# A two-direction Mamba layer and its FFN on one core: the order of convolution, projections and turned steps

## The chip, the cores and the metric

The kernel runs on one core of a Trainium2 chip. TensorE (PE in the profile, PEld its weight loads), VectorE (DVE), ScalarE (ACT), GpSimd (POOL) and SyncE (SP, here the DMA queue) each work off their own instruction stream and wait for each other with semaphores. The metric is the device time of one execution in microseconds (us), the median of several.

## What is computed

The input x has 4 sequences of 512 tokens with 128 features. It is normalised, a Mamba block runs over it forwards and over its reverse, both results are added, normalised again and added to x; then an FFN with int weights (hidden size 384) follows in the same sandwich of layer norms. One Mamba pass, with inner size 256 and 16 states:

```python
xz = einsum('bld,ed->ble', x, in_w); u, z = split(xz, 2)
u = silu(causal depthwise conv of u with 4 taps + conv_b)
x_dbl = einsum('bld,ed->ble', u, xproj_w)      # 8 columns for dt, 16 for B, 16 for C
dt = softplus(x_dbl[..., :8] @ dt_w.T + dt_b)
dA = exp(dt[..., None] * A); dBu = dt[..., None] * B[:, :, None, :] * u[..., None]
h_t = dA_t * h_(t-1) + dBu_t;  y_t = sum over the 16 states of h_t * C_t
y = (y + u * D) * silu(z);  out = y @ out_w.T
```

## The kernel before, in words

**Units and steps.** A unit k is one sequence q = k // 2 in one direction d = k % 2: eight units (UNITS). Each has 16 steps, one for each state (NS); step i of the 128 belongs to unit i // 16 and has position i % 16. A step works on tiles of 128 partitions by 1024: the two halves of the inner size side by side, 512 tokens each. For a step, ScalarE makes the decay `da` with two exponentials (stage "exp"), VectorE runs one scan instruction over decay and input `bb` (stage "scan"), GpSimd multiplies the result `hq` by the row of C (stage "mul_c"), and TensorE sums the state over all 16 steps into the PSUM tile `ysum` by eight transposing matmuls (stage "fold", three slots later, FOLD_LAG).

**Three kinds of step.** They differ in how the input dt * B * u comes about. In a plain step TensorE broadcasts the row of B into PSUM with one matmul ("bcast") and VectorE multiplies it by `dtu` ("mul_b"). In a turned step (table TURNED) ScalarE scales the transposed `dtu_t` by B's columns with four activations ("g") and TensorE turns it back with eight transposes ("g_turn"), so that VectorE has only the scan. In a pooled step (table POOLED) GpSimd does the product from a row of B that a DMA spread over the partitions ("mul_b_pooled"), and ScalarE writes the decay into the PSUM tile ("exp_psum", line 909 on). There are two such PSUM tiles (BB_RING), so the feed of step i + 1 waits for scan i - 1. `da` has six buffers and `hq` five. Scan i also waits for fold i - 5.

**The order.** `plan()` writes one list, ORDER, by hand. Slot i holds scan i, mul_c i, the feed of step i + 1, the exponentials of step i + 5, the stages in `sooner[i]`, fold i - 3, and then those that `put(slot, ...)` appended to `woven[i]`. Slots in the table `late` have their exponentials after the woven stages of the slot named there. Every engine walks through the same list and executes its own stages, so the place in the list is the place in each engine's stream. Between the steps of a unit are woven:

- four taps for each of two halves of the next unit's convolution ("tap", TensorE, line 781), which is done with in-projection weights multiplied by the taps, then "conv_out" (ScalarE, Silu, line 963), which leaves `u` in one of three buffers (U_RING);
- "z" (two matmuls, Silu, line 970); "xproj" (two matmuls, copied to `xdbl`), whose B and C rows SyncE stores to DRAM and loads again, spread, as `c_tiles` and `b_tiles`; "bc", "split" (GpSimd, four small operations) and "b_rows", which prepare B; "dt" (two matmuls, Softplus, line 993) and "dtu" (GpSimd), "dtu_turn" (transposes);
- for the unit that has just ended, "y_out" (ScalarE, slot 2, copies `ysum`), "back" (TensorE adds the skip term and turns y into token order, lines 743 and 748) and "gate" (VectorE multiplies it by `zs`, line 1381);
- in even units from 2 on, out-projection and layer norm 2 of the sequence before; in odd ones from 3 on layer norm 3 and the FFN of it ("ln_square", "ln_var", "ln_pow", "ln_shift", "ln_act", "turn_x1", "ffn_gate", "ffn_up", "ffn_down"). I call these FFN units.

Exp, Silu and Softplus need different activation tables of ScalarE; a table load appears in the profile at the line of the activation behind it.

**Scratch.** All woven matmuls write to two PSUM banks (`scr`). `plan_banks` walks the list and gives each result the bank whose last use ends first, from its first matmul to the stage that reads it; `may_write` makes TensorE wait until the previous holder of the bank has been read.

The stages of unit k before, as offsets to its first slot: taps of unit k + 1 in 0 to 3 with both conv_outs in 3; z in 4; back in 5 and 6, gates in 6 and 7; xproj in 7, bc in 8, dt, split and dtu in 9; b_rows in 10 or 11; FFN gates in 10 and 11. Unit 0 has its convolution three slots later.

Of the kernel before, what the change touches and what calls it, by code (L numbers as in the profile page):

```python
# [27 lines left out]
UNITS = 2 * SEQS  # L28
# [26 lines left out]
TURNED = ((4, 6, 10, 13), (2, 4, 6, 10, 13)) + 3 * ((3, 6, 10, 12, 15), (0, 5, 10, 13))  # L55
POOLED = ((15,), (15,), (8, 14), (15,)) + 2 * ((8, 14), (8, 15))
# [60 lines left out]
def plan():  # L117
# [26 lines left out]
    late = {}  # L144
    for k in range(UNITS):
        q, d, n, at = k // 2, k % 2, k + 1, NS * k
        more, ffn = n < UNITS, d == 1 and q >= 1
        lag = 3 if k == 0 else 0
        g_slot = {2: 0, 3: 0, 4: 1, 5: 1, 6: 2, 10: 6, 12: 9, 13: 8 if ffn else 10, 15: 11}
# [3 lines left out]
        for p in POOLED[k]:  # L153
            put(at + {8: 4, 14: 10, 15: 11}[p], ("mul_b_pooled", at + p))
# [9 lines left out]
        if more:  # L164
            put(at + lag, *taps(n, 0)[:2])
            put(at + lag + 1, *taps(n, 0)[2:])
            put(at + lag + 2, *taps(n, 1)[:2])
            put(at + lag + 3, *taps(n, 1)[2:], ("conv_out", n, 0), ("conv_out", n, 1))
        put(at + lag + 4, ("z", k, 0), ("z", k, 1))
        late[at + lag + 4] = at + lag + 4  # L170

        if k >= 1:
            put(at + 5, ("back", k - 1, 0))
            put(at + 6, ("gate", k - 1, 0), ("back", k - 1, 1))
            put(at + 7, ("gate", k - 1, 1))

        if more:
            then = 1 if k == 0 else 0
            put(at + then + 7, ("xproj_mm", n, 0), ("xproj_mm", n, 1), ("xproj", n))
            put(at + then + 8, ("bc", n))  # L180
            put(at + then + 9, ("dt_mm", n, 0), ("dt_mm", n, 1), ("dt", n, 0), ("dt", n, 1), ("split", n), ("dtu", n))

        if d == 0 and q >= 1:
            for b in range(BLK):
                put(at + 10 + b, ("oproj_mm", q - 1, 0, b))
            put(at + 13, ("oproj", q - 1, 0))
            put(at + 14, ("ln_square", 2, q - 1))
            put(at + 15, ("ln_var", 2, q - 1, 0), ("ln_pow", 2, q - 1, 0))
            put(at + 16, ("ln_act", 2, q - 1, 0), ("add_attn", q - 1, 0))
            put(at + 18, ("ln_square", 3, q - 1))  # L190
            put(at + 19, ("ln_var", 3, q - 1, 0), ("ln_pow", 3, q - 1, 0), ("ln_shift", 3, q - 1, 0))
            put(at + 21, ("ln_act", 3, q - 1, 0))
        if ffn:
            soon = 0 if more else -2
            put(at + soon + 7 + 2 * (not more), ("turn_x1", q - 1, 0))
            put(at + soon + 10, ("ffn_gate", q - 1, 0, 0), ("ffn_gate", q - 1, 0, 1))
            put(at + soon + 11, ("ffn_gate", q - 1, 0, 2))
            late[at + soon + 10] = late[at + soon + 11] = at + soon + 11
# [10 lines left out]
        if more:  # L209
            put(at + (11 if ffn or k == 0 else 10), ("b_rows", n))  # L210
            soon = 1 if d == 0 and k >= 1 else 0
            put(at + 12 - soon, ("dtu_turn", n, 0))
            put(at + 13 - soon, ("dtu_turn", n, 1))
            if q < LAST:
                put(at + 14, ("turn", q + 1, d))
            if 0 in TURNED[n]:
                put(at + 14 - soon, ("g", at + NS))
# [8 lines left out]
    for i in range(STEPS + FOLD_LAG):  # L226
        if i < STEPS:
# [5 lines left out]
            if i + 1 < STEPS and not is_turned(i + 1) and not is_pooled(i + 1):  # L233
                order.append(("mul_b", i + 1))
            if i not in late:
                order += exps(i)
            order += sooner[i]
# [79 lines left out]
def mamba_sandwich(nc, x, packed, conv_taps, w_u, w_ffn, bc_rows, out):  # L317
# [3 lines left out]
    with ExitStack() as ctx:  # L321
# [252 lines left out]
        def _(sp):  # L574
# [13 lines left out]
            for k in range(UNITS):  # L588
# [4 lines left out]
                for m in range(NS // 2):  # L593
# [8 lines left out]
                    for p in POOLED[k]:  # L602
                        if m == {8: 0, 14: 3, 15: 3}[p]:
# [896 lines left out]
```

## Time and profile before

| | |
|---|---|
| time, median of 3 | 470.99 us (468.65 to 473.14) |
| profiled execution | 472.82 us, its span 471.0 us |
| mean granted clock of TensorE | 0.921 of full |
| PE busy | 405.1 us (86%) |
| DVE busy | 422.3 us (90%) |
| ACT busy | 374.3 us (79%) |
| POOL busy | 398.9 us (85%) |
| DMA | 42.6 MB on one hardware queue, 26.4% of 16 engines |

The first scan starts at 23.1 us and the last ends at 439.7; the scans of the units begin at 23.1, 77.1, 126.8, 175.8, 231.0, 278.8, 335.0 and 382.8. What follows the last scan is the last sequence's projection, norms and FFN. In the rows below a stretch A:B is given in us from the span's start, then its length, then for each engine busy us and in brackets the instructions, then TensorE's granted clock as a share of full speed, the DMA engines' share and GB/s. In the time order a line has start, duration, engine, source line, operation and tiles, number of instructions merged, and in square brackets the idle time ahead with what ended it.

### The profile page before, as it was taken

How to read it: one execution, taken by the hardware profiler on the slowest of the kernel's cores; microseconds unless marked ns; L12 is line 12 of the kernel's file. 1: busy time of each engine (PE TensorE's matmuls, PEld its weight loads, DVE VectorE, ACT ScalarE, POOL GpSimd, SP SyncE). 2: the span in 40 equal slices, each digit the busy share in tenths (PEclk: the TensorE clock that was granted, in tenths of full speed). 3: DMA queues.
4: the chain of work that ended last, by engine and by line, in shares of the span. 5: the costliest groups of instructions: out<-in, count | busy, mean ns of one | idle time of the engine just before them, and what ended most of it. 6: DMA issues, size and time to landing. Idle time of an engine off the chain costs nothing. (4 is left out here: it accounts for less than half of the span.)

```text
span 471.0 us, 6668 instructions
## 1 busy us (share of the span) xinstructions
PE 405.1 (86%) x2250; PEld 277.5 (59%) x2250; DVE 422.3 (90%) x338; ACT 374.3 (79%) x732; POOL 398.9 (85%) x239
## 2 busy tenths in 40 slices
PE   7759898997699799789998899889998965879973
PEld 3346476555456684555656775455766854548853
DVE  3998989999999999899999999988999999889744
ACT  4798799798858997998889997997889887863330
POOL 1678999978999799979989999979789999968421
PEclk9958958998899999999999999979998995979978
DMA  8531112322232213231233323122322223210001
GB/s 244 205 147 61 75 66 102 131 82 81 82 118 90 96 46 113 89 97 67 94 110 110 118 89 114 61 100 94 112 87 93 96 89 113 90 45 1 2 0 45
DMA packets 17777, 43.02 MB, mean 91 GB/s; under 512 B 1616, under 2 KB 7120, under 8 KB 17744
## 3 DMA queue, kind: packets, MB, share of 16 engines
q1 hardware_dynamic: 17744, 42.61, 26.4%
q8 instruction: 18, 0.29, 0.3%
q14 instruction: 15, 0.12, 0.1%
HBM read 41.03 MB, written 1.57 MB: 90 GB/s over the span
## 5 line engine op out<-in xcount | busy, mean ns | idle before, releaser
L1123 POOL TENSOR_TENSOR hq<-hq,c_tiles 128x1024 f32<-128x1024 f32 x127 | 298.0, 2366 | 30.6 <-DVE hq L1276 30.3
L1276 DVE TENSOR_TENSOR_SCAN hq<-da,bb 128x1024 f32<-128x1024 f32 x115 | 260.4, 2280 | 9.4 <-PE bb L679 2.9
L909 ACT ACTIVATE da<-dt,neg_a 128x511 f32<-128x511 f32 x230 | 149.8, 711 | 7.4 <-DVE hq L1276 7.2
L707 PE MATMUL ysum<-wts,hq 128*128 128x128 f32 x1024 | 145.9, 290 | 7.7 <-ACT y_t L949 4.9
L707 PEld LDWEIGHTS ysum<-wts,hq 128*128 128x128 f32 x1024 | 121.6, 148 | 32.6 <-issue 19.7
L1257 DVE TENSOR_TENSOR bb<-bb,dtu 128x1024 f32<-128x1024 f32 x79 | 95.8, 1213 | 8.3 <-PE bb L652 7.5
L1020 ACT ACTIVATE g<-dtu_t,bc_t 128x256 f32<-128x256 f32 x144 | 61.0, 498 | 0.0
L679 PE MATMUL bb<-wts,g 128*128 128x128 f32 x288 | 43.2, 300 | 8.0 <-ACT g L1020 5.7
L679 PEld LDWEIGHTS bb<-wts,g 128*128 128x128 f32 x288 | 36.4, 154 | 17.6 <-issue 10.2
L652 PE MATMUL bb<-b_rows,pick 48*128 48x512 bf16 x75 | 29.9, 398 | 10.2 <-DVE hq L1276 10.2
L1276 DVE TENSOR_TENSOR_SCAN hq<-bb,dbu 128x1024 f32<-128x1024 f32 x13 | 29.7, 2281 | 6.7 <-issue 4.3
L652 PEld LDWEIGHTS bb<-b_rows,pick 48*128 48x128 bf16 x75 | 7.0, 93 | 45.1 <-issue 22.5
L781 PE MATMUL scr<-xn_rev,wconv 128*128 128x512 f32 x64 | 32.3, 628 | 0.0
L1135 POOL TENSOR_TENSOR dbu<-dtu,b_tiles 128x1024 f32<-128x1024 f32 x13 | 30.8, 2367 | 0.0
L873 PE MATMUL scr<-x_t,wffn 128*128 128x512 f32 (+1 forms) x46 | 24.5, 639 | 5.3 <-issue 2.7
L781 PE MATMUL scr<-xn_fwd,wconv 128*128 128x512 f32 x56 | 27.1, 609 | 0.0
L1225 POOL TENSOR_TENSOR rstd<-rstd,minus_half 128x4 f32<-128x4 f32 (+1 forms) x15 | 13.8, 922 | 15.0 <-DVE rstd L1397 14.3
L909 ACT ACT_TABLE_LOAD x17 | 21.8, 1283 | 0.4
L970 ACT ACTIVATE zs<-scr 128x512 f32<-128x512 f32 x16 | 9.6, 598 | 12.0 <-PE scr L791 12.0
L791 PE MATMUL scr<-xn_fwd,wts 128*128 128x512 f32 x32 | 15.2, 597 | 2.7 <-ACT u L963 2.7
L781 PEld LDWEIGHTS scr<-xn_rev,wconv 128*128 128x128 f32 x64 | 11.8, 206 | 9.4 <-issue 9.4
L1212 POOL TENSOR_TENSOR dtu<-dt,u 128x1024 f32<-128x1024 f32 x7 | 16.5, 2362 | 0.6 <-ACT dt L993 0.5
(150 smaller groups left out, 489.8 us busy)
## 6 DMA issues: line engine op xcount, KB each, us to landing
c_tiles<-bc_rows_dram SPq DMA_DIRECT2D x64, 512.0 KB, 3.6
b_tiles<-bc_rows_dram SPq DMA_DIRECT2D x13, 256.0 KB, 4.4
x_res<-x_dram SPq DMA_DIRECT2D x1, 768.0 KB, 8.1
out_dram<-o SPq DMA_DIRECT2D x3, 256.0 KB, 2.3
wts<-packed_dram SPq DMA_DIRECT2D x1, 584.0 KB, 9.1
hid<-w_ffn_dram SPq DMA_DIRECT2D x1, 576.0 KB, 7.8
wconv<-conv_taps_dram SPq DMA_DIRECT2D x2, 256.0 KB, 4.4
wconv<-conv_taps_dram SPq DMA_DIRECT2D x1, 512.0 KB, 7.6
```

The lines of the kernel that those rows point to most:

```text
L652: mm = nc.tensor.matmul(bb[:, i % BB_RING, 1, :], pick[0:PARTS * NS, n:n + 1].broadcast_to([PARTS * NS, P]), b_rows[:, k % 2, :], start=Tr ...
L679: mm = nc.tensor.matmul(bb[:, i % BB_RING, h, block(b)], g[:, n % G_RING, b, h, :], ident, start=True, stop=True, is_transpose=True)
L707: mm = nc.tensor.matmul(ysum[:, bank, at], hq[:, i % H_RING, h, block(b)], ident, start=opens, stop=(i % NS == NS - 1), is_transpose=True, ...
L781: mm = nc.tensor.matmul(scratch(use), wconv[:, d, t, h * P:(h + 1) * P], src, start=(t == 0), stop=(t == TAPS - 1))
L873: signal_full(nc.tensor.matmul(scratch(use)[:, 0:at.stop - at.start], w[:, block(c)], x1_t[:, at], start=True, stop=True), use)
L909: ins = nc.scalar.activation(da[:, i % DA_RING, h, 1:SEQ], dt[:, k % 2, h, 1:SEQ], ACT.Exp, scale=neg_a[:, c:c + 1])
L1020: ins = nc.scalar.activation(g[:, m % G_RING, b], dtu_t[:, k % 2, b], ACT.Copy, scale=bc_t[:, k % 2, b, ROW_B + n:ROW_B + n + 1])
L1123: nc.gpsimd.tensor_tensor(hq[:, i % H_RING], hq[:, i % H_RING], c_tiles[:, n % C_RING, i % 2, :].unsqueeze(1).broadcast_to([P, 2, SEQ]), A ...
L1135: nc.gpsimd.tensor_tensor(dbu[:], dtu[:, k % 2], b_tiles[:, n % POOLED_RING].unsqueeze(1).broadcast_to([P, 2, SEQ]), ALU.mult).then_inc(s_ ...
L1212: nc.gpsimd.tensor_tensor(dtu[:, k % 2], dt[:, k % 2], u[:, k % U_RING], ALU.mult).then_inc(s_dtu, 1)
L1257: nc.vector.tensor_tensor(bb[:, i % BB_RING], bb[:, i % BB_RING, 1, :].unsqueeze(1).broadcast_to([P, 2, SEQ]), dtu[:, k % 2], ALU.mult).th ...
L1276: nc.vector.tensor_tensor_scan(out=hq[:, i % H_RING].rearrange("p h t -> p (h t)"), data0=decay.rearrange("p h t -> p (h t)"), data1=dbu_t ...
```

## The change

The tables have six turned steps a unit from unit 2 on (3, 5, 7, 10, 12, 15 in even units, 0, 3, 5, 7, 10, 13 in odd ones) and one pooled step (14 or 15). The convolution of unit k + 2 is put into slots 3 to 6 of unit k, for k from 2 to 5; unit 0 makes that of unit 1, unit 1 those of units 2 and 3. From unit 2 on xproj is in slot 0, bc and split in slot 1, b_rows in slot 2, back in slots 3 and 4, gates in 4 and 5, z in slot 7, and dt in slot 8, or 9 in FFN units. There the exponentials of slots 7 to dt's come behind dt. The FFN gates stand in slots 8 and 9, the turn of x1 in `sooner` of slot 7, which now comes ahead of the slot's exponentials, and LN 3's stages in slots 3, 4 and 6. The transposes of x and their evaluation ("turn") move to an earlier unit accordingly. SyncE loads the row of the pooled step behind the fourth pair of C rows in all units.

```diff
--- before.py
+++ after.py
@@ -52,8 +52,8 @@
 PARTS = 3
-TURNED = ((4, 6, 10, 13), (2, 4, 6, 10, 13)) + 3 * ((3, 6, 10, 12, 15), (0, 5, 10, 13))
-POOLED = ((15,), (15,), (8, 14), (15,)) + 2 * ((8, 14), (8, 15))
+TURNED = ((4, 6, 10, 13), (2, 4, 6, 10, 13)) + 3 * ((3, 5, 7, 10, 12, 15), (0, 3, 5, 7, 10, 13))
+POOLED = ((15,), (15,)) + 3 * ((14,), (15,))
 POOLED_RING = 2
@@ -142,16 +142,23 @@
                           (3 * NS + 9, "attn_in", 3)):
         put(slot, (name, q))
     late = {}
+
+    def conv_ahead(slot, n):
+
+        put(slot, *taps(n, 0)[:2])
+        put(slot + 1, *taps(n, 0)[2:])
+        put(slot + 2, *taps(n, 1)[:2])
+        put(slot + 3, *taps(n, 1)[2:], ("conv_out", n, 0), ("conv_out", n, 1))
+
     for k in range(UNITS):
         q, d, n, at = k // 2, k % 2, k + 1, NS * k
         more, ffn = n < UNITS, d == 1 and q >= 1
-        lag = 3 if k == 0 else 0
-        g_slot = {2: 0, 3: 0, 4: 1, 5: 1, 6: 2, 10: 6, 12: 9, 13: 8 if ffn else 10, 15: 11}
+        g_slot = {2: 0, 3: 0, 4: 1, 5: 2, 6: 2, 7: 4, 10: 6 if k < 2 else 5, 12: 9, 13: 10, 15: 11}
         for p in TURNED[k]:
             if p:
                 put(at + g_slot[p], ("g", at + p))
         for p in POOLED[k]:
-            put(at + {8: 4, 14: 10, 15: 11}[p], ("mul_b_pooled", at + p))
+            put(at + {14: 10, 15: 11}[p], ("mul_b_pooled", at + p))
         if k == 0:
             put(at, ("dtu_turn", 0, 0), ("dtu_turn", 0, 1), ("pick",), ("split", 0), ("turn", 0, 1))
             put(at + 1, ("b_rows", 0))
@@ -161,41 +168,46 @@
             put(at + 8, ("down_sum",))
             put(at + 11, ("down_centre",))
+        if k <= 1:
+            conv, z_slot, back, xproj, bc = (at + 2 - 2 * k, at + 6 - 2 * k, at + 5, at + 7 - 2 * k, at + 8 - k)
+            conv_ahead(conv, n)
+        else:
+            z_slot, back, xproj, bc = at + 7, at + 3, at, at + 1
+        dt_slot = at + (9 if k == 0 else 10 if k == 1 else 9 if ffn else 8)
+        put(z_slot, ("z", k, 0), ("z", k, 1))
+        if k <= 1:
+            late[z_slot] = z_slot
+            if k == 1:
+                late[dt_slot] = dt_slot
+        else:
+            for s in range(at + 7, dt_slot + 1):
+                late[s] = dt_slot
+
+        if k >= 1:
+            put(back, ("back", k - 1, 0))
+            put(back + 1, ("gate", k - 1, 0), ("back", k - 1, 1))
+            put(back + 2, ("gate", k - 1, 1))
+        if k >= 1 and k + 2 < UNITS:
+            conv_ahead(at + (6 if k == 1 else 3), k + 2)
+
         if more:
-            put(at + lag, *taps(n, 0)[:2])
-            put(at + lag + 1, *taps(n, 0)[2:])
-            put(at + lag + 2, *taps(n, 1)[:2])
-            put(at + lag + 3, *taps(n, 1)[2:], ("conv_out", n, 0), ("conv_out", n, 1))
-        put(at + lag + 4, ("z", k, 0), ("z", k, 1))
-        late[at + lag + 4] = at + lag + 4
-
-        if k >= 1:
-            put(at + 5, ("back", k - 1, 0))
-            put(at + 6, ("gate", k - 1, 0), ("back", k - 1, 1))
-            put(at + 7, ("gate", k - 1, 1))
-
-        if more:
-            then = 1 if k == 0 else 0
-            put(at + then + 7, ("xproj_mm", n, 0), ("xproj_mm", n, 1), ("xproj", n))
-            put(at + then + 8, ("bc", n))
-            put(at + then + 9, ("dt_mm", n, 0), ("dt_mm", n, 1), ("dt", n, 0), ("dt", n, 1), ("split", n), ("dtu", n))
-
+            put(xproj, ("xproj_mm", n, 0), ("xproj_mm", n, 1), ("xproj", n))
+            put(bc, ("bc", n), ("split", n))
         if d == 0 and q >= 1:
             for b in range(BLK):
                 put(at + 10 + b, ("oproj_mm", q - 1, 0, b))
             put(at + 13, ("oproj", q - 1, 0))
             put(at + 14, ("ln_square", 2, q - 1))
             put(at + 15, ("ln_var", 2, q - 1, 0), ("ln_pow", 2, q - 1, 0))
-            put(at + 16, ("ln_act", 2, q - 1, 0), ("add_attn", q - 1, 0))
-            put(at + 18, ("ln_square", 3, q - 1))
-            put(at + 19, ("ln_var", 3, q - 1, 0), ("ln_pow", 3, q - 1, 0), ("ln_shift", 3, q - 1, 0))
-            put(at + 21, ("ln_act", 3, q - 1, 0))
+            put(at + 17, ("ln_act", 2, q - 1, 0), ("add_attn", q - 1, 0))
         if ffn:
+            put(at + 3, ("ln_square", 3, q - 1))
+            put(at + 4, ("ln_var", 3, q - 1, 0), ("ln_pow", 3, q - 1, 0), ("ln_shift", 3, q - 1, 0))
+            put(at + 6, ("ln_act", 3, q - 1, 0))
             soon = 0 if more else -2
-            put(at + soon + 7 + 2 * (not more), ("turn_x1", q - 1, 0))
-            put(at + soon + 10, ("ffn_gate", q - 1, 0, 0), ("ffn_gate", q - 1, 0, 1))
-            put(at + soon + 11, ("ffn_gate", q - 1, 0, 2))
-            late[at + soon + 10] = late[at + soon + 11] = at + soon + 11
+            sooner[at + 7].append(("turn_x1", q - 1, 0))
+            put(at + 8, ("ffn_gate", q - 1, 0, 0), ("ffn_gate", q - 1, 0, 1))
+            put(at + 9, ("ffn_gate", q - 1, 0, 2))
             for c in range(3):
                 sooner[at + soon + 12 + c].append(("ffn_up_mm", q - 1, 0, c))
                 put(at + soon + 12 + c, ("ffn_up", q - 1, 0, c))
@@ -207,12 +219,16 @@
             put(at + soon + 20, ("ln_act", 4, q - 1, 0), ("add_ffn", q - 1, 0))
         if more:
-            put(at + (11 if ffn or k == 0 else 10), ("b_rows", n))
+            put(dt_slot, ("dt_mm", n, 0), ("dt_mm", n, 1), ("dt", n, 0), ("dt", n, 1), ("dtu", n))
+            put(at + (2 if k >= 2 else 11), ("b_rows", n))
             soon = 1 if d == 0 and k >= 1 else 0
             put(at + 12 - soon, ("dtu_turn", n, 0))
-            put(at + 13 - soon, ("dtu_turn", n, 1))
-            if q < LAST:
-                put(at + 14, ("turn", q + 1, d))
+            put(at + 13, ("dtu_turn", n, 1))
+            if k == 0:
+                put(at + 13, ("turn", 1, 0))
+                put(at + 14, ("turn", 1, 1))
+            elif k + 3 < UNITS:
+                put(at + 14, ("turn", (k + 3) // 2, (k + 3) % 2))
             if 0 in TURNED[n]:
                 put(at + 14 - soon, ("g", at + NS))
     put(STEPS - 5, ("oproj_part_mm",), ("oproj_part",))
@@ -232,9 +248,9 @@
                 order.append(("g_turn" if is_turned(i + 1) else "exp_psum" if is_pooled(i + 1) else "bcast", i + 1))
             if i + 1 < STEPS and not is_turned(i + 1) and not is_pooled(i + 1):
                 order.append(("mul_b", i + 1))
+            order += sooner[i]
             if i not in late:
                 order += exps(i)
-            order += sooner[i]
         f = i - FOLD_LAG
         last_in_slot = f >= NS and f % NS == 0
@@ -600,7 +616,7 @@
                                                                                       ).partition_broadcast(P)
                                  ).then_inc(s_cl[n % C_RING], 16)
                     for p in POOLED[k]:
-                        if m == {8: 0, 14: 3, 15: 3}[p]:
+                        if m == 3:
                             n = pooled_steps(NS * k + p)
                             if n >= POOLED_RING:
```

## Rows read from the trace of the kernel before

**Rows 1.** Stretches (units 4, 5): us; PE, PEld, DVE, ACT, POOL busy; clock; DMA.

```profile
231.00:279.00 48.00, 44.08 (x287) 32.10 (x286) 46.33 (x27) 43.16 (x89) 46.03 (x26) 1.00 0.31 105
...
279.00:335.00 56.00, 51.33 (x265) 31.95 (x263) 51.53 (x33) 49.20 (x97) 53.01 (x32) 0.94 0.29 96
```

**Rows 2.** Groups by line on the page: busy us, mean ns, idle before.

```profile
L1020 ACT ACTIVATE g<-dtu_t,bc_t 128x256 f32<-128x256 f32 x144 | 61.0, 498 | 0.0
...
L1135 POOL TENSOR_TENSOR dbu<-dtu,b_tiles 128x1024 f32<-128x1024 f32 x13 | 30.8, 2367 | 0.0
...
L909 ACT ACT_TABLE_LOAD x17 | 21.8, 1283 | 0.4
```

**Rows 3.** Waits of VectorE: engine, line, releaser; us, times, longest.

```profile
DVE bb L1257 <- PE bb L652: 7.5, 9, 1.9
...
DVE hq L1276 <- issue: 4.3, 3, 1.8
...
DVE hq L1276 <- ACT bb L920: 2.4, 3, 0.9
```

**Rows 4.** VectorE in order of time: start us, us, what, idle before.

```profile
138.56 1.23 DVE L1257 TENSOR_TENSOR bb<-bb,dtu 128x1024 f32<-128x1024 f32 x1 [0.29 <-PE bb L652]
...
196.20 1.23 DVE L1257 TENSOR_TENSOR bb<-bb,dtu 128x1024 f32<-128x1024 f32 x1 [1.90 <-PE bb L652]
...
297.79 1.23 DVE L1257 TENSOR_TENSOR bb<-bb,dtu 128x1024 f32<-128x1024 f32 x1 [0.54 <-PE bb L652]
...
299.12 2.29 DVE L1276 TENSOR_TENSOR_SCAN hq<-da,bb 128x1024 f32<-128x1024 f32 x1
...
301.32 1.21 DVE L1257 TENSOR_TENSOR bb<-bb,dtu 128x1024 f32<-128x1024 f32 x1
...
302.43 0.68 DVE L1381 TENSOR_TENSOR gated<-scr,zs 128x512 f32<-128x512 f32 x1
...
307.67 2.29 DVE L1276 TENSOR_TENSOR_SCAN hq<-bb,dbu 128x1024 f32<-128x1024 f32 x1 [1.78 <-issue]
...
320.02 1.23 DVE L1257 TENSOR_TENSOR bb<-bb,dtu 128x1024 f32<-128x1024 f32 x1 [0.77 <-PE bb L652]
...
324.19 0.69 DVE L1432 TENSOR_TENSOR hid<-scr,hid 128x512 f32<-128x512 f32 x1 [0.56 <-PE scr L873]
```

**Rows 5.** TensorE in order of time, unit 5.

```profile
285.81 0.39 PE L652 MATMUL bb<-b_rows,pick 48*128 48x512 bf16 x1
...
286.13 1.09 PE L707 MATMUL ysum<-wts,hq 128*128 128x128 f32 x8
...
287.06 1.88 PE L781 MATMUL scr<-xn_fwd,wconv 128*128 128x512 f32 x4
...
288.87 0.39 PE L652 MATMUL bb<-b_rows,pick 48*128 48x512 bf16 x1
...
292.84 1.04 PE L679 MATMUL bb<-wts,g 128*128 128x128 f32 x8
...
293.71 1.04 PE L707 MATMUL ysum<-wts,hq 128*128 128x128 f32 x8
...
298.61 1.02 PE L743 MATMUL scr<-u,skip_diag 128*128 128x512 f32 x2
...
300.01 0.39 PE L652 MATMUL bb<-b_rows,pick 48*128 48x512 bf16 x1
```

**Rows 6.** ScalarE in order of time, unit 5.

```profile
294.65 1.26 ACT L963 ACTIVATE u<-scr,wts 128x512 f32<-128x512 f32 x2
...
298.08 1.28 ACT L909 ACT_TABLE_LOAD   x1
...
299.38 2.56 ACT L909 ACTIVATE da<-dt,neg_a 128x511 f32<-128x511 f32 x4
...
301.84 1.64 ACT L1055 ACTIVATE ln_tile<-x_res,shift,rstd 128x128 f32<-128x128 f32 x4
```

**Rows 7.** The emptiest stretch of TensorE in unit 7, same columns as rows 1.

```profile
389.00:395.00 6.00, 1.65 (x10) 0.90 (x9) 5.82 (x4) 5.50 (x13) 6.00 (x4) 0.58 0.47 131
```

## The prediction

> **What bounds the kernel now.** I read the stretches by unit first, because the program is eight units of sixteen steps and an average over the span hides which unit has slack. In the stretch of unit 4 VectorE is busy 46.3 of 48 us, in unit 5 51.5 of 56 [rows 1]. GpSimd follows at 46.0 and 53.0. So the even units already run at VectorE's pace; what is left is idle time of VectorE in the odd ones. A step costs VectorE one scan, 2.20 us from its start to the next instruction's, and a plain step a product more, 1.3 us (297.79 to the scan at 299.12); a gate adds 0.6, its 0.68 less the overlap [rows 4].
>
> The groups by line give the prices [rows 2], the list of waits says what VectorE waits for [rows 3]: broadcasts of B by TensorE (7.5 us in nine waits), decays that ScalarE writes into PSUM for a pooled step (2.4 in three), and 4.3 us in three waits without a releaser. The time order places them [rows 4]: 1.90 us in unit 3 and 0.54 in unit 5, both at step 6, right behind the slots that hold convolution and z; 0.29 at the same step of unit 2; 0.77 in unit 5 behind the first FFN matmuls and 0.56 at the first up product; 1.78 ahead of the pooled step 8 of unit 5, one of the three without releaser.
>
> **Work removed from VectorE.** Counting the tables, turned steps go from 36 to 45, pooled from 13 to 8, plain from 79 to 75. Four products fewer on the engine that sets the pace, at 1.3 us: **-5.2 us** (two in unit 3, one each in 5 and 7).
>
> **Pooled step 8 goes.** All three waits without releaser stand ahead of step 8 (units 2, 5, 7). The product by GpSimd had long been ready, so I read them as ScalarE being late with a decay that cannot be made ahead, since it needs one of the two PSUM tiles. **-4.3 us.** Step 14 stays pooled in even units, and so do its waits (2.4); I leave them, and put them at nought only in the low case. GpSimd loses five products of 2.367 us, 11.8 in all; it sets no VectorE wait in rows 3, so I count nothing, but it is what gives GpSimd room for the shorter odd units: 53.0 busy of 56 in unit 5 would otherwise stand above VectorE's.
>
> **ScalarE.** A turned step needs four scalings: 144 took 61.0 us, so 1.69 us a step, and nine more are +15.2. A pooled step's two exponentials cost what a plain one's do. Table loads take 1.283 us each [rows 2]; the 17 into Exp stand there. By the order, before, a unit with a successor has Silu, Exp, Softplus, Exp (4), an FFN unit one more Silu, unit 7 four; that is 34. After, units 0 and 1 have 4 and 5, units 2 to 6 three each (Silu, Softplus, Exp), unit 7 two: 26. Eight fewer are -10.3. Net +4.9 us on an engine busy 43.2 of 48 and 49.2 of 56 [rows 1]. Hidden by VectorE's 48 us; nothing. If that cover were gone, 0.7 us a unit.
> The row shows a load starting at 298.08 and the next exponential at 299.38, 1.30 us later [rows 6]. The Trainium skill (ScalarE: Activation LUTs, What ACT_TABLE_LOAD costs) adds a drain of about 1.38 us to each switch. By it eight loads would be worth 21 us and ScalarE would end with less work than before. Here the row decides: no such drain is seen.
>
> **TensorE, where the change costs.** Nine more turns back at 0.87 us (292.84 to 293.71) against four broadcasts of 0.32: about +6.6 us of work, but its place matters more. Pitches from start to start [rows 5]: broadcast 0.32 (285.81), fold 0.93 (286.13), two taps 1.81 (287.06), back 1.40 (298.61 to 300.01), turn 0.87. Today taps lie in slots 0 to 3 and back in 5 to 7. From unit 2 on, slots 3 to 6 hold both, and two of the steps fed there, 5 and 7, become turned, so that the slots before them are short. Slot 3: 0.32+0.93+1.40+1.81 = 4.5. Slot 4: 0.87+0.87+1.40+1.81 = 5.0. Slot 5: 0.32+0.93+1.81 = 3.1. Slot 6: 0.87+0.87+1.81 = 3.6. Sum 16.1. VectorE's time in the same slots, scans of 2.2, two products (1.3), two gates (0.6): 3.5+2.8+4.1+2.2 = 12.6. TensorE can run behind by one scan (2.2 us) before VectorE waits, because two PSUM tiles alternate. From the start of scan 3 to the product of step 8 VectorE has 14.8 us of work; TensorE's broadcast for it is done at 16.1+0.4. So at least **1.7 us** of waiting in each of units 2 to 5.
> There are also waits inside. Scratch has two banks. With the taps of half 0 holding one from slot 3 to 6, back of half 1 must wait until VectorE's gate of half 0 has read the other (slot 4), and the taps of half 1 until the gate of half 1 has (slot 5). Followed from scan 3 at 0: turn for step 5 done at 5.2, back 1 from 6.3, broadcast 6 at 9.8, so the product of step 6 starts 1.4 late; its gate ends at 11.8, taps until 13.6, turn 7 at 14.5 (0.6 late); broadcast 8 at 17.4 (0.7 late). **2.7 us** a unit, four units: **+10.8**. I take this one, since the gates' waits follow from the order. It replaces 1.90, 0.54 and 0.29 [rows 4]: **-2.7**. Behind the waiting matmul on TensorE stand the next feed and fold, so VectorE is the one who waits.
>
> **FFN units.** x1 is now turned early in slot 7, and its input, LN 3's scaling, stands on ScalarE behind the second conv_out. A Silu half is 0.6 us, the scaling 1.64 [rows 6]: TensorE sits some 2.1 us, then x1's turn (0.6), fold, z (1.81) and the broadcast follow: step 9's product starts 2.2 us late. Dt behind three gate matmuls in slot 9 may add 1.1. Units 3 and 5: **+4.4** (between 0 and +6.6). It replaces waits behind the FFN matmuls in unit 5, 0.77 and 0.56: **-1.3**. Unit 7 has no convolution; its waits I leave.
>
> **Smaller moves.** xproj in slot 0, bc and split in slot 1, b_rows in slot 2 lie where no taps are now: 0.32+0.93+1.81 is under a plain slot's 3.5. SyncE's store of the rows stands behind the unit's C loads in its queue as before, so it moves at most a few us earlier; split moves past GpSimd's products of slots 2 to 9 and adds none. Nothing for either. Postponed exponentials of slots 7 to 9 are those of steps 12 to 14, needed three slots later: nothing. Units 0 and 1 get other slots at the same work: nothing, +-1.
>
> **Sum.** -5.2 -4.3 -2.7 -1.3 +10.8 +4.4 = +1.7 us. The profiled execution took 472.8 us for its span of 471.0; the median of the runs is 471.0. 471.0+1.7: **472.7, called 472.5**.
>
> **Rivals.**
> *TensorE keeps up* (faster). If only the unavoidable 1.7 a unit shows (+6.8) and the x1 turn is on time (0): -13.5+6.8 = -6.7, 464; with step 14's waits gone as well, -9.1, 462. For it: ScalarE loses loads and GpSimd a product a unit, and folds could then fall in earlier. Against it: both stalls come from the written order, not from a loaded engine. Chance 0.31.
> *The dense stretch costs its full price* (slower). One mechanism: TensorE in slots 3 to 9 of units 2 to 5. With dt's 1.1 also paid (+2.2) and slots 3 and 4 partly run at half rate, 1.7 us a unit (+6.8), +10.7: 481. It decides from about 1.5 us more a unit than my 2.7. The clock side is seen in the trace: in 389 to 395 TensorE is busy 1.65 of 6 us and the granted clock is 0.58 of full, that is part of it at 1.2 in place of 2.4 GHz [rows 7]; the taps that fill slots 0 to 2 today leave them, and slot 1 will hold 1.7 us of 3.5. Against it: xproj and b_rows fill some, and the drop at 389 came after emptier slots. Chance 0.27.
> The Trainium skill (TensorE: Matmul & The Clock Gate, HAM oscillation) says that an array left idle for a while between bursts goes back to half rate and starts each burst cold. The stretch of [rows 7] agrees for unit 7; for units 2 to 5 it would give the 481, and I put 0.10 of the 0.27 on it.
> *The change does not do what it says* (a bank or a semaphore serialises TensorE so that the visits of ScalarE are split again): then loads stay near 34 and the time lies within the slower case.
>
> **Numbers.** Forecast (within 1%, about what a measurement of this kernel can tell from no change) 0.42, its own range 467 to 475.5; faster 0.31; slower 0.27, the third rival inside it. Range 461 to 480: the low end is the first rival's full case, the high end cuts the last of the second's.
>
> **What would show it.** Right: VectorE waits for TensorE's broadcast at steps 6 and 8 and its turn at 7 in units 2 to 5, some 2.7 us together, and at step 9 in units 3 and 5; TensorE's weight loads waiting for `gated`; 45 turned groups, 8 fewer table loads; no wait ahead of step 8. Wrong: units 2 to 5 shorter than before with no waits in slots 5 to 9 (TensorE had more room than the pitches say), or a clock below 1.0 in slots 3 to 6, or waits for GpSimd's C products, which would make it the bound of units 3 and 5.

## The result and the profile after

The changed kernel takes **499.3 us** (median; 498.9 to 500.1) against 471.0; the ratio is 1.060 (95% interval 1.055 to 1.066). The forecast was 472.5, its range 461 to 480, with 0.27 on slower. The profiled execution has a span of 497.2 us, 26.2 more than before.

Busy time by engine, part 1 of the page of the kernel after (us, share of the span, instructions):

```profile
PE 418.4 (84%) x2318; PEld 288.9 (58%) x2318; DVE 418.9 (84%) x334; ACT 378.1 (76%) x755; POOL 388.0 (78%) x234
```

No engine has much more work: VectorE 3.4 us less, GpSimd 10.9 less, ScalarE 3.8 more, TensorE 13.3 more. So the 26 us are idle time of the engine that sets the pace. Groups by line on the same page, which answer to [rows 2]; the number behind the bar's second place is the idle time ahead:

```profile
L1139 POOL TENSOR_TENSOR hq<-hq,c_tiles 128x1024 f32<-128x1024 f32 x127 | 298.4, 2367 | 62.2 <-DVE hq L1292 62.1
...
L925 ACT ACTIVATE da<-dt,neg_a 128x511 f32<-128x511 f32 x240 | 156.2, 715 | 2.7 <-DVE hq L1292 2.5
...
L1273 DVE TENSOR_TENSOR bb<-bb,dtu 128x1024 f32<-128x1024 f32 x75 | 91.1, 1215 | 29.3 <-PE bb L668 29.2
L1036 ACT ACTIVATE g<-dtu_t,bc_t 128x256 f32<-128x256 f32 x180 | 76.6, 503 | 1.6 <-PE bb L695 1.1
...
L1151 POOL TENSOR_TENSOR dbu<-dtu,b_tiles 128x1024 f32<-128x1024 f32 x8 | 19.0, 2372 | 0.0
```

The counts are those forecast: 75 products, 180 scalings (45 steps), 8 pooled products. Table loads fell from 39 to 31, into Exp from 17 to this:

```profile
L925 ACT ACT_TABLE_LOAD x11 | 14.1, 1283 | 0.3
```

GpSimd waits twice as long for VectorE (62.1 us) as before, so it is further from setting the time. The list of waits of VectorE and of TensorE in the kernel after (us in total, times, longest), to be held against [rows 3]:

```profile
DVE bb L1273 <- PE bb L668: 29.2, 24, 3.2
DVE hid L1448 <- PE scr L889: 8.4, 2, 4.2
DVE hq L1292 <- PE bb L695: 6.5, 6, 2.3
```

```profile
PE bb L695 <- ACT g L1036: 17.5, 9, 5.2
PE scr L682 <- POOL b_parts L1216: 10.4, 6, 2.7
PE scr L797 <- DVE gated L1397: 3.9, 4, 1.0
```

I then went along VectorE's time order and added its idle times of 0.2 us and more between the first and the last scan, by unit and by step:

| waits of VectorE, us | before | after |
|---|---|---|
| unit 0; unit 1 | 3.6; 0.3 | 0.3; 4.5 |
| steps 4 to 8 of units 2 to 5, but for pooled steps | 2.7 | 21.3 |
| step 9 of units 3 and 5 | 0 | 5.2 |
| step 11 of units 3 and 5 | 0 | 3.2 |
| steps 12 and 13 of units 2 to 6 | 1.8 | 15.5 |
| pooled steps 8; 14 | 4.3; 2.4 | 0; 0 |
| unit 7 without its pooled step | 3.8 | 0.4 |
| step 0 of unit 5 | 0 | 0.4 |
| sum | 18.9 | 50.7 |

31.8 more waits less 5.2 of products are 26.6; from the first to the last scan it took 27.7 us more, and the tail 1.3 less. The units took, before, 54.0, 49.7, 49.0, 55.2, 47.8, 56.2, 47.8 and (to the last scan's start) 54.7 us; after, 49.9, 54.5, 56.0, 64.4, 54.5, 66.1, 49.4 and 47.3. So units 1 to 6 lose 39.1 us and the two ends give back 11.5.

Unit 4 after, VectorE in order of time (start us, us, what, idle before), where [rows 4] has such rows of before:

```profile
260.36 2.29 DVE L1292 TENSOR_TENSOR_SCAN hq<-da,bb 128x1024 f32<-128x1024 f32 x1
262.56 0.67 DVE L1397 TENSOR_TENSOR gated<-scr,zs 128x512 f32<-128x512 f32 x1
264.69 2.29 DVE L1292 TENSOR_TENSOR_SCAN hq<-da,bb 128x1024 f32<-128x1024 f32 x1 [1.46 <-PE bb L695]
268.85 1.23 DVE L1273 TENSOR_TENSOR bb<-bb,dtu 128x1024 f32<-128x1024 f32 x1 [1.87 <-PE bb L668]
...
273.74 2.29 DVE L1292 TENSOR_TENSOR_SCAN hq<-da,bb 128x1024 f32<-128x1024 f32 x1 [0.87 <-issue]
276.59 1.23 DVE L1273 TENSOR_TENSOR bb<-bb,dtu 128x1024 f32<-128x1024 f32 x1 [0.57 <-PE bb L668]
```

These are scan 5, the product of step 6, scan 7 and the product of step 8: the places forecast, at 1.87, 0.87 and 0.57 for 1.4, 0.6 and 0.7, and 1.46 at step 5 that was not. TensorE shows where that one begins, in slot 2:

```profile
257.23 0.40 PE L682 MATMUL scr<-ident,b_parts 128*48 128x128 bf16 x4 [1.68 <-POOL b_parts L1216]
...
257.88 1.73 PE L759 MATMUL scr<-u,skip_diag 128*128 128x512 f32 x2
259.41 1.06 PE L764 MATMUL scr<-wts,y_t 128*128 128x128 f32 x4
```

It stands at b_rows until GpSimd has split B, the broadcast for step 4 queued behind it, and the back that follows takes 2.4 us in place of 1.4. The clock was granted at half (1.2 of 2.4 GHz) for a part of this stretch:

```profile
256.00:262.00 6.00, 4.77 (x14) 2.55 (x15) 5.91 (x4) 6.00 (x14) 5.69 (x8) 0.72 0.23 87
```

Unit 5 after, ScalarE, TensorE and VectorE around steps 11 to 13:

```profile
345.87 1.09 ACT L1009 ACTIVATE dt<-scr 128x512 f32<-128x512 f32 x2
...
346.98 1.28 ACT L925 ACT_TABLE_LOAD   x1
...
348.27 3.78 ACT L925 ACTIVATE da<-dt,neg_a 128x511 f32<-128x511 f32 x6
...
351.96 1.69 ACT L1036 ACTIVATE g<-dtu_t,bc_t 128x256 f32<-128x256 f32 x4
...
353.70 1.97 PE L695 MATMUL bb<-wts,g 128*128 128x128 f32 x8 [4.12 <-ACT g L1036]
...
357.48 0.69 DVE L1448 TENSOR_TENSOR hid<-scr,hid 128x512 f32<-128x512 f32 x1 [4.22 <-PE scr L889]
```

Dt is late, the table load follows, then the three postponed pairs of exponentials, and only then the scaling for step 13. (Slot 10 has no pair of its own, since step 15 is pooled here.) TensorE waits 4.1 us for the scaling, with the FFN's up matmul behind the turn in its queue, and VectorE 4.2 us for that matmul. The granted clock is 0.67 of full from 345 to 351 us and 0.50 from 351 to 357, and the turn behind the wait takes 1.97 us where one at full clock took 1.04 [rows 5]. The profile names the FFN at the end of this chain; its cause is ScalarE's order.

### The profile page after: what moved, and what is told of

It reads as the page before. It is cut to its first block and busy times, and to the rows that moved or that the text cites. A ratio compares the mean times of both kernels' runs of the same rounds, so it can differ in the third digit from the quotient of the medians.

```text
span 497.2 us, 6835 instructions
## 1 busy us (share of the span) xinstructions
PE 418.4 (84%) x2318; PEld 288.9 (58%) x2318; DVE 418.9 (84%) x334; ACT 378.1 (76%) x755; POOL 388.0 (78%) x234
## 5 line engine op out<-in xcount | busy, mean ns | idle before, releaser
L1139 POOL TENSOR_TENSOR hq<-hq,c_tiles 128x1024 f32<-128x1024 f32 x127 | 298.4, 2367 | 62.2 <-DVE hq L1292 62.1
L1292 DVE TENSOR_TENSOR_SCAN hq<-da,bb 128x1024 f32<-128x1024 f32 x120 | 272.2, 2281 | 18.4 <-PE bb L695 6.5
L925 ACT ACTIVATE da<-dt,neg_a 128x511 f32<-128x511 f32 x240 | 156.2, 715 | 2.7 <-DVE hq L1292 2.5
L1273 DVE TENSOR_TENSOR bb<-bb,dtu 128x1024 f32<-128x1024 f32 x75 | 91.1, 1215 | 29.3 <-PE bb L668 29.2
L1036 ACT ACTIVATE g<-dtu_t,bc_t 128x256 f32<-128x256 f32 x180 | 76.6, 503 | 1.6 <-PE bb L695 1.1
L695 PE MATMUL bb<-wts,g 128*128 128x128 f32 x360 | 52.9, 295 | 25.5 <-ACT g L1036 17.5
L695 PEld LDWEIGHTS bb<-wts,g 128*128 128x128 f32 x360 | 44.0, 151 | 38.4 <-ACT g L1036 26.1
L979 ACT ACTIVATE u<-scr,wts 128x512 f32<-128x512 f32 x16 | 10.8, 687 | 23.4 <-PE scr L797 21.5
L1151 POOL TENSOR_TENSOR dbu<-dtu,b_tiles 128x1024 f32<-128x1024 f32 x8 | 19.0, 2372 | 0.0
L1292 DVE TENSOR_TENSOR_SCAN hq<-bb,dbu 128x1024 f32<-128x1024 f32 x8 | 18.2, 2271 | 0.4 <-ACT bb L936 0.4
L1024 ACT ACTIVATE dtu_t<-scr 128x512 f32<-128x512 f32 x16 | 9.4, 591 | 11.2 <-PE scr L703 11.2
```

The costliest lines, as they stand in the source:

```text
L695: mm = nc.tensor.matmul(bb[:, i % BB_RING, h, block(b)], g[:, n % G_RING, b, h, :], ident, start=True, stop=True, is_transpose=True)
L925: ins = nc.scalar.activation(da[:, i % DA_RING, h, 1:SEQ], dt[:, k % 2, h, 1:SEQ], ACT.Exp, scale=neg_a[:, c:c + 1])
L1036: ins = nc.scalar.activation(g[:, m % G_RING, b], dtu_t[:, k % 2, b], ACT.Copy, scale=bc_t[:, k % 2, b, ROW_B + n:ROW_B + n + 1])
L1139: nc.gpsimd.tensor_tensor(hq[:, i % H_RING], hq[:, i % H_RING], c_tiles[:, n % C_RING, i % 2, :].unsqueeze(1).broadcast_to([P, 2, SEQ]), A ...
L1151: nc.gpsimd.tensor_tensor(dbu[:], dtu[:, k % 2], b_tiles[:, n % POOLED_RING].unsqueeze(1).broadcast_to([P, 2, SEQ]), ALU.mult).then_inc(s_ ...
L1273: nc.vector.tensor_tensor(bb[:, i % BB_RING], bb[:, i % BB_RING, 1, :].unsqueeze(1).broadcast_to([P, 2, SEQ]), dtu[:, k % 2], ALU.mult).th ...
```

## Experiments

Each run names a theory that the trace after had not settled. The two main ones: **order** (where the stages stand) and **tables** (nine more turned steps load TensorE and ScalarE).

**Order alone.** The order after, the tables before; the product of the pooled step 8 is then in slot 4 and its row of B is loaded first, as before:

```diff
-TURNED = ... + 3 * ((3, 5, 7, 10, 12, 15), (0, 3, 5, 7, 10, 13))
+TURNED = ... + 3 * ((3, 6, 10, 12, 15), (0, 5, 10, 13))
-POOLED = ((15,), (15,)) + 3 * ((14,), (15,))
+POOLED = ((15,), (15,), (8, 14), (15,)) + 2 * ((8, 14), (8, 15))
```

Expected: 

> The order of the changed kernel with the step tables of the kernel before (36 turned, 13 pooled, 79 plain). Theory 'order': the loss comes from where convolution, back, gates, dt and the postponed exponentials stand, so the kernel stays slow, 488 to 502 us; it has 5.2 us more products on VectorE but longer slots. Theory 'tables': the nine extra turned steps load TensorE and ScalarE; without them it is near the kernel before, 468 to 476 us.

Measured: 507.0 us, ratio to before 1.080 (1.072 to 1.089). Worse than the whole change, and above the range given for either theory; so in the new order the new tables are worth 7.7 us. The waits at steps 4 to 7 are there, and the pooled steps 8 wait far longer than in [rows 4], since ScalarE's exponentials for them now follow conv_out and, in unit 5, LN 3's scaling (unit 5, VectorE; in units 2 and 4 it is 2.58 us each):

```profile
343.65 2.29 DVE L1292 TENSOR_TENSOR_SCAN hq<-bb,dbu 128x1024 f32<-128x1024 f32 x1 [4.10 <-ACT bb L936]
```

**Tables alone.** The order before, the tables after (in the kernel before); the scaling for step 7 is put into slot 4:

```diff
-TURNED = ... + 3 * ((3, 6, 10, 12, 15), (0, 5, 10, 13))
+TURNED = ... + 3 * ((3, 5, 7, 10, 12, 15), (0, 3, 5, 7, 10, 13))
-POOLED = ((15,), (15,), (8, 14), (15,)) + 2 * ((8, 14), (8, 15))
+POOLED = ((15,), (15,)) + 3 * ((14,), (15,))
```

Expected: 

> The order of the kernel before with the new step tables (45 turned, 8 pooled, 75 plain). Theory 'order': near the kernel before, 463 to 474 us (5.2 us of products and 4.3 us of waits at step 8 gone, some waits for TensorE added). Theory 'tables': most of the 28 us loss is here, 488 us or more.

Measured: 471.7 us, ratio 1.003 (0.999 to 1.006). So the loss is the order's. But in the old order the tables bring nothing either: what they take from VectorE comes back largely where ScalarE's scaling for step 3 is late in odd units, with TensorE behind it. ScalarE, TensorE and VectorE in unit 5:

```profile
285.24 1.28 ACT L1052 ACTIVATE ln_tile<-o,rstd 128x128 f32<-128x128 f32 x4 [2.47 <-POOL rstd L1225]
...
288.17 1.09 PE L679 MATMUL bb<-wts,g 128*128 128x128 f32 x8 [2.57 <-ACT g L1020]
...
289.36 2.29 DVE L1276 TENSOR_TENSOR_SCAN hq<-da,bb 128x1024 f32<-128x1024 f32 x1 [1.57 <-ACT da L909]
...
293.90 1.23 DVE L1257 TENSOR_TENSOR bb<-bb,dtu 128x1024 f32<-128x1024 f32 x1 [2.25 <-PE bb L652]
```

The scaling stands behind that of layer norm 2 in slot 0, for which ScalarE waits 2.47 us on GpSimd's `rstd`. The change moved layer norm 2's scaling (`ln_act`) one slot later, and in the changed kernel ScalarE waits for `rstd` nowhere in these units.

**Scaling ahead of the postponed exponentials**, in the changed kernel:

```diff
-        g_slot = {..., 12: 9, 13: 10, 15: 11}
+        g_slot = {..., 12: 9 if k < 2 else 7, 13: 10 if k < 2 else 7, 15: 11}
```

Expected: 

> The changed kernel with one edit: from unit 2 on the scaling for step 12 or 13 is written in slot 7, ahead of z, dt and the postponed exponentials, in place of slots 9 and 10. Theory 'scaling late': the waits at steps 12 and 13 of units 2 to 6 (15.5 us by the trace) shrink to those of the decays themselves, so 484 to 491 us. Theory 'ScalarE is full there': what is taken from the scaling comes back as waits for the decays of steps 12 to 14, and the time stays within 3 us of 499.

Measured: 490.5 us, 8.8 less. The waits at steps 12 and 13 fall from 15.5 to 0.5 us; in unit 3 step 13's 4.2 us are gone:

```profile
233.64 0.67 DVE L1448 TENSOR_TENSOR hid<-scr,hid 128x512 f32<-128x512 f32 x1
234.22 2.27 DVE L1292 TENSOR_TENSOR_SCAN hq<-da,bb 128x1024 f32<-128x1024 f32 x1
```

Not all 15 us reach the end: at steps 4 and 5 of units 3 and 5 the waits grew from 3.3 to 11.1 us, where TensorE's wait for the split grew:

```profile
PE scr L682 <- POOL b_parts L1216: 13.9, 6, 4.6
```

In unit 4 the opposite happened, and it separates two things that the changed kernel has together. TensorE waited for the split as long as there (1.67 us for 1.68), but the clock stayed at full:

```profile
253.94 0.40 PE L682 MATMUL scr<-ident,b_parts 128*48 128x128 bf16 x4 [1.67 <-POOL b_parts L1216]
```

```profile
252.70:258.70 6.00, 4.76 (x25) 2.90 (x26) 5.91 (x4) 6.00 (x14) 5.69 (x8) 1.00 0.27 87
```

The back behind it took 1.4 us instead of 2.4, and VectorE's wait at step 5 is 0 for 1.46. So a wait of this length for the split costs VectorE nothing there at full clock; the 1.46 us of the changed kernel appear only with the half clock. In units 3 and 5 the split's wait is 3.25 and 4.56 us and the clock falls as well, so that their parts can't be told apart.

**Split and b_rows late again**, in the changed kernel:

```diff
-            put(bc, ("bc", n), ("split", n))
+            put(bc, ("bc", n))
+            put(bc if k < 2 else at + 9, ("split", n))
-            put(at + (2 if k >= 2 else 11), ("b_rows", n))
+            put(at + 11, ("b_rows", n))
```

Expected: 

> The changed kernel with one edit: from unit 2 on split stands in slot 9 and b_rows in slot 11, as in the kernel before, in place of slots 1 and 2. Theory 'TensorE enters the dense stretch late because it waits for GpSimd's split': the 10 us of TensorE's waits for it fall away, with them 0.6 to 0.8 us at step 4 and a part of the waits at steps 5 and 6 of units 2 to 5, 488 to 495 us. Theory 'the stretch is too dense by itself': 497 to 500 us.

Measured: 492.6 us, 6.7 less. The waits at steps 4 and 5 are gone, and what stays in each of units 2 to 5 is the forecast's own pattern, here unit 4:

```profile
262.97 1.23 DVE L1274 TENSOR_TENSOR bb<-bb,dtu 128x1024 f32<-128x1024 f32 x1 [1.56 <-PE bb L669]
...
267.86 2.29 DVE L1293 TENSOR_TENSOR_SCAN hq<-da,bb 128x1024 f32<-128x1024 f32 x1 [0.87 <-issue]
270.71 1.23 DVE L1274 TENSOR_TENSOR bb<-bb,dtu 128x1024 f32<-128x1024 f32 x1 [0.57 <-PE bb L669]
```

1.56 + 0.87 + 0.57 = 3.0 us a unit, against 2.7 worked out. TensorE's clock is at full in slots 1 to 7 of all four units here, so the 6.7 us are the split and the clock together.

**Both edits**, the two diffs above together.

Expected: 

> The changed kernel with both edits: scaling for step 12 or 13 in slot 7, split in slot 9 and b_rows in slot 11. Theory 'independent causes': the gains add, 8.8 and 6.7 us, so 482 to 486 us, and what stays are the waits of the dense stretch at steps 6 to 8 (3.0 us in each of units 2 to 5) and those at steps 9 and 11 of units 3 and 5. Theory 'one cause': both removed the same lateness, and the time is 488 us or more.

Measured: 479.5 us, ratio 1.021 (1.016 to 1.026): 19.9 less than the change, more than the 15.6 of the two apart, and under the range of either theory (the four runs lie between 475.9 and 481.8). They are not independent: with the scaling alone moved, the waits at steps 4 and 5 of units 3 and 5 had grown by 7.8 us, and the late split takes these too.

**LN 3 a slot earlier as well:**

```diff
-            put(at + 3, ("ln_square", 3, q - 1))
+            put(at + 2, ("ln_square", 3, q - 1))
...
-            put(at + 6, ("ln_act", 3, q - 1, 0))
+            put(at + 5, ("ln_act", 3, q - 1, 0))
```

Expected: 

> Those two edits and LN 3's stages one slot earlier (2, 3 and 5), so that its scaling stands ahead of conv_out on ScalarE. Theory 'x1's turn waits for the scaling behind conv_out': the wait at step 9 of units 3 and 5 (3.3 to 3.6 us each) falls by about 2, together 3 to 5 us under the run with two edits. Theory 'ScalarE or TensorE is full in slots 7 to 9': no change within 1.5 us.

Measured: 476.3 us (ratio 1.011, 1.007 to 1.015), 3.2 less by the medians, though the runs of the two kernels overlap. The wait at step 9 is gone in units 3 and 5, and so is TensorE's for the scaling; before this edit they were, in unit 5,

```profile
318.87 0.65 PE L879 MATMUL scr<-wts,ln_tile 128*128 128x128 f32 x4 [1.99 <-ACT ln_tile L1072]
...
324.17 1.23 DVE L1274 TENSOR_TENSOR bb<-bb,dtu 128x1024 f32<-128x1024 f32 x1 [3.28 <-PE bb L669]
```

In unit 3, at full clock, the wait at step 9 was 1.95; in unit 5 the granted clock is 0.72 of full from 318 to 324 us, and z behind x1's turn takes 3.28 us there for 1.88 in unit 3, so the clock has a part in the larger wait. The trace kept of this run is of one of its two fastest executions (last section), so its waits flatter it against the median.

The wait at step 11 stayed at 1.6 and 1.4. TensorE works without idle time ahead of it, the gate matmuls and dt's four (1.87 us) last; I take it for work packed too densely, but no run took it away.

**Half of the taps left out.** Two of the four taps of each convolution from unit 4 on are not computed, on top of the first two edits:

```diff
-        return [("tap", k, h, t) for t in range(TAPS)]
+        return [("tap", k, h, t) if k < 4 or t % 3 == 0 else None for t in range(TAPS)]
```

Expected: 

> The two edits, and from unit 4 on two of the four taps of each convolution are left out, so TensorE has 0.9 us less in each of slots 3 to 6 of units 2 to 5. Theory 'TensorE is too dense there': with 3.6 us less work against a wait of 3.0 us, the waits at steps 6 to 8 vanish but for what the gates' bank waits hold (up to 1 us a unit), 8 to 13 us under the run with two edits. Theory 'the gates' banks serialise it': most of the 3.0 us a unit stays, less than 5 us gained.

Measured: 468.7 us, 10.8 less. The 3.0 us a unit are 0.7, unit 4:

```profile
250.62 1.23 DVE L1274 TENSOR_TENSOR bb<-bb,dtu 128x1024 f32<-128x1024 f32 x1 [0.71 <-PE bb L669]
...
252.36 4.58 DVE L1293 TENSOR_TENSOR_SCAN hq<-da,bb 128x1024 f32<-128x1024 f32 x2
```

So the stretch is mostly a matter of TensorE's work a slot. The banks, for which it waits 0.98 us in each of four units with all the taps and with half of them, may hold the 0.7 that is left; no run took them away.

**Only the end units.** The kernel before, with unit 0's convolution, z, xproj, bc and dt a slot earlier and unit 7 laid out as in the change, but for layer norms 2 and 3, which keep their old slots:

```diff
-        lag = 3 if k == 0 else 0
+        lag = 2 if k == 0 else 0
+        end = k == UNITS - 1
...
-        put(at + lag + 4, ("z", k, 0), ("z", k, 1))
+        put(at + (7 if end else lag + 4), ("z", k, 0), ("z", k, 1))
...
+            back = at + (3 if end else 5)
```

Expected: 

> The kernel before, with only the two end units changed: unit 0 has convolution, z, xproj, bc and dt one slot earlier, and unit 7 has the changed kernel's layout and steps (turned 0, 3, 5, 7, 10, 13; back in 3 and 4, z in 7, one visit of ScalarE's Silu table). Theory 'the dense stretch needs a convolution': unit 7, which has none, keeps its 7.5 us gain and unit 0 some 2 us, so 459 to 464 us. Theory 'the gain of unit 7 came from what unit 6 hands over without a convolution': less than 3 us, 467 to 471.

Measured: **464.3 us** (464.0 to 464.6), ratio 0.989 (0.987 to 0.992): faster than both kernels, and just above the first theory's range. Unit 0 takes 49.7 us for 54.0, unit 7 50.6 to the last scan's start for 54.7; unit 1 gives back 1.7. Unit 7 to the end of its last scan, before, after and in this run (the columns are those of [rows 1]):

```profile
382.70:439.80 57.10, 45.76 (x262) 33.88 (x261) 50.74 (x33) 37.58 (x85) 48.71 (x26) 0.85 0.19 61
```

```profile
417.60:467.20 49.60, 41.72 (x277) 31.52 (x276) 48.85 (x31) 37.89 (x90) 43.40 (x24) 1.00 0.18 62
```

```profile
379.80:432.80 53.00, 44.43 (x280) 33.54 (x279) 49.15 (x32) 37.92 (x90) 46.41 (x25) 0.94 0.22 65
```

Unit 7 keeps 4.0 of its 7.4 us although unit 6 still holds its convolution. In the 3.3 us by which it stays behind the changed kernel's stands a wait of VectorE of 2.39 us at step 3. It is the one of the tables alone: the scaling for step 3 stands behind layer norm 2's, which the change has a slot later.

```profile
386.58 1.28 ACT L1063 ACTIVATE ln_tile<-o,rstd 128x128 f32<-128x128 f32 x4 [3.09 <-POOL rstd L1236]
...
389.50 1.97 PE L690 MATMUL bb<-wts,g 128*128 128x128 f32 x8 [5.45 <-ACT g L1031]
```

The mean granted clock is 0.94 of full for 1.00, and the turn behind that wait runs at half; no run had the one without the other.

**Step 8 turned in units 3 and 5 too:**

```diff
-TURNED = ... + 2 * ((3, 6, 10, 12, 15), (0, 5, 10, 13)) + ...
-POOLED = ((15,), (15,), (8, 14), (15,), (8, 14), (8, 15), (8, 14), (15,))
+TURNED = ... + 2 * ((3, 6, 10, 12, 15), (0, 5, 8, 10, 13)) + ...
+POOLED = ((15,), (15,)) + 3 * ((8, 14), (15,))
```

Expected: 

> The kernel with only the end units changed, and in units 3 and 5 step 8 turned (0, 5, 8, 10, 13 turned, 15 pooled), its scaling in slot 5. Theory 'a pooled step needs ScalarE in time': the wait of 1.8 us at step 8 of unit 5 goes and unit 3 has a product of 1.3 us less on VectorE, 461 to 463 us. Theory 'every further turned step is given back by TensorE or ScalarE', as with the tables alone: 464 us or more.

Measured: 467.6 us (ratio 0.995, 0.993 to 0.998), 3.3 more than with the ends alone (ratio 0.989). The theory that it would gain fell: the pooled step taken away was paid back in VectorE's waits for TensorE, unit 5:

```profile
299.96 1.23 DVE L1268 TENSOR_TENSOR bb<-bb,dtu 128x1024 f32<-128x1024 f32 x1 [3.08 <-PE bb L663]
...
313.23 1.23 DVE L1268 TENSOR_TENSOR bb<-bb,dtu 128x1024 f32<-128x1024 f32 x1 [1.98 <-PE bb L663]
```

The first of these begins on ScalarE. A step that is not pooled has its exponentials made ahead, so a pair for step 8 now stands in slot 3, in front of conv_out, and z on TensorE waits for conv_out:

```profile
292.88 1.32 ACT L920 ACTIVATE da<-dt,neg_a 128x511 f32<-128x511 f32 x2
294.22 1.28 ACT L974 ACT_TABLE_LOAD   x1
...
296.35 3.04 PE L802 MATMUL scr<-xn_fwd,wts 128*128 128x512 f32 x4 [1.96 <-ACT u L974]
```

With the ends alone that pair is not there, TensorE waits 0.73 us and z takes 1.96, at full clock; here the granted clock is 0.63 of full while z runs.

**LN 3 behind conv_out in it**, from the even unit's slots 18, 19 and 21 (2, 3 and 5 of the odd one) to the odd one's 3, 4 and 6:

```diff
-            put(at + 18, ("ln_square", 3, q - 1))
...
+            put(at + 3, ("ln_square", 3, q - 1))
```

Expected: 

> The same with LN 3's stages in slots 3, 4 and 6 in place of 2, 3 and 5 in all FFN units, behind conv_out. Theory 'conv_out is late on ScalarE behind LN 3's squares, and z on TensorE behind it': the waits at step 6 of units 3 and 5 (1.9 and 0.5 us) shrink, 1 to 3 us under the run before. Theory 'the scaling then comes late for x1's turn in slot 7': the gain is given back at steps 7 to 9, within 1 us or slower.

Measured: 468.8 us (ratio 0.995, 0.991 to 0.998). The wait at step 6, 3.6 and 3.1 us in the run before it (the 1.9 and 0.5 of the expectation are those with the ends alone), fell to 0.3 and 0.2, which bears out that conv_out was late behind LN 3's squares too. It came back at steps 12 (2.4 us in both units) and 13 (1.4 and 1.5), and in unit 7 the waits grew by 2.7; step 9 waits 1.2 each for 1.0 and 2.0. So nothing is gained.

## Why the prediction was wrong

The largest error is in **"Postponed exponentials of slots 7 to 9 are those of steps 12 to 14, needed three slots later: nothing."** I asked when the decays are needed and not what is queued behind them on ScalarE. That is the scaling of step 12 or 13, and behind its turn on TensorE the FFN's up matmul: 15.5 us of waits, and 8.8 us of time by the experiment that moved the scaling. The term stood at nothing in the sum.

The second is in **"Smaller moves": split "adds none"**, b_rows in slot 2 "nothing". TensorE waits in order. In slot 2 it stands for GpSimd's four small operations just ahead of the stretch that I had found to be too dense, so its one scan of slack is spent, or partly spent, before slot 3. The experiment that moved them back gained 6.7 us, and both edits together 19.9; without these two placements the time is 479.5, inside the range's upper end. How much of the 6.7 is the wait itself is open: the clock drop of that stretch went with it, and in unit 4 of the run with the early scaling a wait of 1.67 us at full clock cost nothing at steps 4 and 5.

The **dense stretch** was right in its mechanism and, with the split out of the way, in its size: 3.0 us a unit for 2.7, and half the taps took away 2.3 of it. In the changed kernel itself steps 4 to 8 wait 5.3 us a unit (21.3 us where the sum had 10.8), because TensorE enters the stretch late and, in units 2, 4 and 5, partly at half clock (0.73, 0.72 and 0.72 of full in the 6 us around). I had put 1.0 of the 2.7 on the banks; with half the taps 0.7 of 3.0 is left, so density makes most of it.

**FFN units**: 4.4 forecast at step 9, 5.2 measured, and the x1 chain shown by the run that moved LN 3: TensorE waits 1.99 us for the scaling in each, for 2.1 forecast. Dt's 1.1 a unit was left to the bounds; the wait at step 11, where dt stands, is 1.6, but no run shows that it is dt's.

**Work removed, pooled step 8**: right. 75 products, no wait at step 8, and those at step 14 vanished too. But the run with the tables alone shows that this gain does not survive in the old order, where layer norm 2 makes the scaling for step 3 late; in the new order the tables were worth 7.7 us.

**ScalarE**: the difference in loads was right (eight fewer), though they are 39 and 31, not 34 and 26; the net is 3.8 us for 4.9. "Hidden" was right for the sum and wrong for the order. The drain of the Trainium skill (ScalarE: Activation LUTs, What ACT_TABLE_LOAD costs) is not seen after either: the load at 346.98 starts 0.02 us behind the end of the Softplus, and to the next exponential at 348.27 are 1.29 us. Over both traces 32 of 39 and 25 of 31 loads have 1.29 or 1.30 us to the next activation.

**Units 0 and 1, "nothing, +-1"**: unit 0 gained 4.1 us and unit 1, with two convolutions, lost 4.8. **Unit 7**, whose waits I left, gained 7.4.

Of the rivals the slower one had part of the place right, the waits at steps 4 to 11, and was too small; the 13.7 us more at steps 12 and 13 lie outside it. Its clock side was seen: in units 2 and 4 step 5 waits 2.28 and 1.46 us, with a granted clock of 0.73 and 0.72, one of the signs that I had named for being wrong. The rule of the Trainium skill that it drew on (TensorE: Matmul & The Clock Gate, HAM oscillation) fits these two units, where the clock is low behind TensorE's wait for the split. It did not hold in unit 4 of the run with the early scaling, where the clock stayed at full behind the same wait. That pair puts unit 4's 1.46 us on the clock; its share in the other units stays open. Open too is what makes up the wait at step 11. The third rival did not occur: loads fell as the order says.

## What to carry to other kernels

When a stage is postponed on an engine, price what stands behind it in that engine's order, not only its own deadline; an average busy share says nothing on that. Ahead of a stretch that is already too dense for one engine, give that engine nothing that waits for another. And look at the parts of a change by unit: here two of eight units held a gain that the other six hid.

## What the hardware showed that I had not expected

The kernel with three edits falls into two groups of times without any change to it: 470.6 and 470.7 us with a mean granted clock of 0.956 of full, and 475.1 to 476.9 with 0.931 to 0.938. The kernel before spreads the same way: executions of 467.9 to 468.4 us had 0.938 to 0.942, those of 472.4 to 473.1 had 0.918 to 0.925. Worked out from the means, an estimate, the slower group spends some 20 us more at half clock, and takes 4.4 to 6.4 us longer. That is as much as some of the edits here gained, so two such kernels are to be compared by several executions and with the clock beside the time. Whether the lower clock makes these executions longer, or longer waits go ahead of the lower clock, is not shown.
